# Moving one DMA, one mean and one sum in a convolution kernel whose two main engines are nearly equal

## The reference, cut to what matters

```python
xp = log_pooling(x)      # 12 masks of 9x9 (averages over rings and sectors), stacked as a 4x3 block per pixel
out = conv(xp, w_conv1, stride=(4, 3))        # so: 12 products of 256x256 per pixel
out = out + conv(x, w_center) + b_center      # 1x1, the pixel itself
mean = out.mean(axis=(0, 2, 3)); var = out.var(axis=(0, 2, 3))
out = (out - mean) * rsqrt(var + 1e-5) * gamma + beta
return relu(out + x)                           # x: 32 images, 256 channels, 28 x 28, float32
```

## Time and profile before

| What | us |
|---|---|
| Median of 3 runs | 1618.82 (1618.82 to 1619.4) |
| The profiled execution, its own time | 1618.86 |
| Its span, first to last instruction | 1617.2 |
| TensorE (PE) busy | 1461.5 |
| VectorE (DVE) busy | 1443.0 |
| ScalarE (ACT) busy | 658.6 |
| POOL busy | 121.0 |

### The profile page before, as it was taken

One profiled execution on the slowest core, in us unless ns is written; L12 is line 12 of the kernel. 1 busy time (PEld: TensorE's weight loads), 2 busy tenths in 40 slices (PEclk: granted clock), 3 DMA queues, 4 the chain that ended last, 5 costly groups with the idle time before them and its releaser, 6 DMA issues.

```text
span 1617.2 us, 22814 instructions
## 1 busy us (share of the span) xinstructions
PE 1461.5 (90%) x8518; PEld 1458.7 (90%) x8518; DVE 1443.0 (89%) x1327; ACT 658.6 (41%) x721; POOL 121.0 (7%) x160
## 2 busy tenths in 40 slices
PE   9999999999999999999999999999999999993000
PEld 9899999999999999999999999999999999993000
DVE  8999999999999999999999999999999999996432
ACT  3334444444333444434343344433434344444432
POOL 1000000000000000000000000000000000000000
PEclk9999999999999999999999999999999999996555
DMA  7355555565455555555545555455554566579999
GB/s 222 88 133 140 144 129 129 131 147 131 122 120 134 147 137 128 127 133 140 131 113 123 145 146 136 125 127 139 137 126 110 132 147 158 155 237 424 425 425 402
DMA packets 65352, 268.76 MB, mean 166 GB/s; under 512 B 7616, under 2 KB 7616, under 8 KB 65344
## 3 DMA queue, kind: packets, MB, share of 16 engines
q1 hardware_dynamic: 39744, 160.53, 30.3%
q0 software_dynamic: 20736, 82.45, 25.7%
q10 hardware_dynamic: 4864, 25.69, 3.8%
HBM read 218.07 MB, written 50.58 MB: 166 GB/s over the span
## 4 chain that ended last, share of the span: by engine, by line
PE 83%; DVE 5%; DMA 4%; ACTq 3%; ACT 3%; issue 1%; SPq 0%; DVEq 0%; POOLq 0%
PE acc L724 28%; PE acc L725 28%; PE acc L723 28%; ACTq L462 3%; ACT phase L459 2%; DMA phase<-y_dram 2%; DVE phase L467 1%; DMA ends<-x_wide 1%; DVE pooled_split L468 1%; DMA row<-x_wide 1%; DMA out<-phase 1%; ACT m_copy L416 0%; DVE y_stage L467 0%; DVE inner_split L468 0%; DVE row L467 0%
## 5 line engine op out<-in xcount | busy, mean ns | idle before, releaser
L398 ACT ACTIVATE pooled_split<-phase 128x1456 fp32r<-128x1456 f32 x192 | 274.1, 1428 | 637.7 <-DVE phase L467 637.2
L468 DVE TENSOR_TENSOR pooled_split<-phase,pooled_split 128x1456 fp32r<-128x1456 f32 x192 | 315.1, 1668 | 0.3 <-ACT pooled_split L398 0.3
L723 PE MATMUL acc<-pooled_split,w_first 128*128 128x364 f32 x768 | 252.3, 329 | 1.5 <-DVE pooled_split L468 1.4
L724 PE MATMUL acc<-pooled_split,w_first 128*128 128x364 f32 x768 | 252.9, 329 | 0.0
L725 PE MATMUL acc<-pooled_split,w_first 128*128 128x364 f32 x768 | 252.8, 329 | 0.0
L725 PE MATMUL acc<-pooled_split,w_outer 128*128 128x364 f32 x768 | 252.7, 329 | 0.0
L723 PE MATMUL acc<-pooled_split,w_outer 128*128 128x364 f32 x768 | 252.1, 328 | 0.5 <-DVE pooled_split L468 0.5
L724 PE MATMUL acc<-pooled_split,w_outer 128*128 128x364 f32 x768 | 252.5, 329 | 0.0
L723 PE MATMUL acc<-inner_split,w_inner 128*128 128x392 f32 (+1 forms) x640 | 216.4, 338 | 3.0 <-DVE w_inner L510 3.0
L723 PE MATMUL acc<-inner_split,w_first 128*128 128x392 f32 (+1 forms) x640 | 217.8, 340 | 0.7 <-DVE inner_split L468 0.5
L725 PE MATMUL acc<-inner_split,w_inner 128*128 128x392 f32 (+1 forms) x640 | 217.3, 340 | 0.0
(11 more groups left out here) (82 smaller groups left out, 2222.6 us busy)
## 6 DMA issues: line engine op xcount, KB each, us to landing
row<-x_wide SPq DMA_DIRECT2D x64, 558.0 KB, 3.7
row<-x_wide POOLq DMA_DIRECT2D x64, 558.0 KB, 7.5
ends<-x_wide SPq DMA_DIRECT2D x64, 504.0 KB, 3.9
ends<-x_wide POOLq DMA_DIRECT2D x64, 504.0 KB, 6.5
x_pad<-x SPq DMA_DIRECT2D x64, 392.0 KB, 3.1
y_dram<-y_stage SPq DMA_DIRECT2D x31, 784.0 KB, 5.5
phase<-y_dram SPq DMA_DIRECT2D x30, 784.0 KB, 23.6
out<-phase ACTq DMA_DIRECT2D x30, 784.0 KB, 33.3
```

Source lines behind the costliest of these rows:

```text
L398: nc.scalar.activation(view(pooled_split, 2 * j * PAIR, (1, PAIR)), view(phase2, POOLED_LOW + 2 * j * PAIR, (1, PAIR)), ACT.Copy)\
L468: sub = lambda out_, a, b: nc.vector.tensor_tensor(out_, a, b, ALU.subtract)
L723: nc.tensor.matmul(place, hi_w, hi_in, start=start, stop=False)
L724: nc.tensor.matmul(place, lo_w, hi_in, start=False, stop=False)
```

## The change

Three edits. The first image's ends load now goes out ahead of the outer weights of c = 0 and ahead of SP's wait for row2_ready. The pivot is made by ScalarE in the first half of image 1 (image_steps with second=True), with two passes of the function Identity, scale -1/784 and accum_out, one for each output group, and the four measure passes of image 0 stand where those of later images do. And in second halves three_columns is called ahead of lo_of_sums, for all images but the first.

```diff
@@ the loads before the loops
             begin_sum(0, 0, row2, W + 3, row2_begun)
+            begin_sum(0, 0, ends, W, ends_begun)
+            sp.wait_ge(row2_ready, 16)
             load_weights(0, 1)
-            sp.wait_ge(row2_ready, 16)
-            begin_sum(0, 0, ends, W, ends_begun)
             load_x(0, 1)
@@ ScalarE
+            def make_pivot():
+
+                for o in range(CH):
+                    act.wait_ge(y_ready, o + 1 + FREE)
+                    wait_from_one(act, pivot_ready, o)
+                    nc.scalar.activation(view(m_copy, 0, (1, HW)), view(y_stage, o * HW, (1, HW)), ACT.Identity,
+                                         scale=-1.0 / HW, accum_out=minus_pivot[:, o:o + 1])\
+                        .then_inc(pivot_ready, 1)
@@ ScalarE, image_steps
-                    if c == 1 and not first and not second:
+                    if c == 1 and not first:
                         measure(image - 1, 1)
...
                     for j in range(PAIRS):
                         split_pooled(s, j)
-                        if second and c == 1 and j > 0:
-                            measure(image - 1, j - 1)
-                    if c == 0 and not first and not second:
+                    if second and c == 0:
+                        make_pivot()
+                    if c == 0 and not first:
                         measure(image - 1, 0)
@@ VectorE, image_steps
                     if c == 0:
                         take_middle(image - 1)
-                    lo_of_sums(s)
-                    three_columns(image, c)
+                        lo_of_sums(s)
+                        three_columns(image, c)
+                    else:
+                        three_columns(image, c)
+                        lo_of_sums(s)
                     lo_of_shifted(s)
...
-                    if second and c == 1:
-                        make_pivot()
                     third_sum(s)
```

More of the change, by code:

```diff
@@ L153, in x_slot_whole @@
             return view(phase2, (2 * d - 1) * PLACE, (HW, CH), (1, HW))
-        pivot_stats = sb("pivot_stats", CH * 2 * 6)
-        pivot_moments = sb("pivot_moments", CH * 2)
         minus_pivot = sb("minus_pivot", CH)
@@ L409, in copy_middle @@
                         .then_inc(m_copied, 1)
+            def make_pivot():
[5 more added lines that the diff above has]
+                        .then_inc(pivot_ready, 1)
             def measure(image, o):
                 act.wait_ge(y_ready, CH * image + o + 1 + FREE)
-                act.wait_ge(pivot_ready, 1)
+                act.wait_ge(pivot_ready, CH)
                 for kind, function in enumerate((ACT.Identity, ACT.Square)):
@@ L531, in take_y @@
                     add(y, view(acc, 2 * o * BANK, (BANK, 2), (H, U), (1, H)), y).then_inc(y_ready, 1)
[L533 to L543, removed]
             def pooled_place(s, j, first, *dims):
@@ L689, in _ @@
             dve.wait_ge(params_loaded, 48)
-            dve.wait_ge(pivot_ready, 1)
+            dve.wait_ge(pivot_ready, CH)
             link(sub(mean[:, :], totals[:, 0:CH], minus_pivot[:, :]))
```

## The result

The changed kernel takes 1624.63 us (median of 8 runs, 1622.8 to 1627.37) against 1619.32 for the kernel before (8 runs): a ratio of 1.0033, 95% interval [1.0023, 1.0044], or 5.3 us slower (forecast: 4.3 slower). Its profiled execution took 1627.37 us, the slowest of the eight, with a span of 1625.7.

What follows compares the result with a forecast made beforehand. TensorE and VectorE shared the lead; VectorE, with 1.02 us to spare per image, would become the loop's bound. TensorE's end moves from 1468.4 to 1472.7: 1618.86 + 4.3 = 1623.2 us, range 1616.8 to 1628.0.

Steps and rivals of the forecast that it cites:

- Third edit: Second halves: a 1.58 us wait for inner_split becomes about 2.8 us for row sums; VectorE bounds the loop.
- The step of take_y: From image 2 on, VectorE's take_y stands about 45.25 us apart, against TensorE's 45.08.
- L - S: Second halves: landing of the accumulated row sums (L) minus start of the last differences instruction, phase<-d (S); mean 3.70 us.
- rival A: Loop: TensorE stays the bound from mean L - S of 3.53 down; not slower, 1616.9 to 1617.8 us; chance 0.27.
- Rival B: Loop: row sums land early enough not to be waited for (L - S about 2.5); faster, 1615.2 us; chance 0.03.
- First edit: Start: ends lands before VectorE needs it, gaining 2.05 us (0.9 to 2.05); the later outer weights cost 0.
- Rival D: Start: the outer weight piece is late by up to 1.1 us, carried to the end, 1624.3 us; chance 0.06.
- the sign of D: Start: ScalarE's first pooled split starting later than 21.8 us would show that the outer weight piece was late.
- Second edit: Image 1, first half: mean on ScalarE takes 2.97 and 0.31 us off VectorE; cost 0 with 0.7 us spare.
- The sum: Whole kernel: take_y of image 2 at 115.66, then 29 cycles, to TensorE's end at 1472.7 against 1468.4, +4.3 us.
- the hole in TensorE adds nothing: Image 1, second half: TensorE finds lo_of_sums done only at 91.5 us, but VectorE doesn't wait for TensorE; cost 0.
- wait for inner_split in nearly every image: Loop: TensorE would wait for inner_split in nearly every image, a few tenths of a us at a time.

Runs made afterwards that it cites:

- e3: Changed kernel with SP's store of y_stage moved from the first half into the second half, behind the x load; 1616.06 us, ratio 0.9981 to the kernel before.
- e8: Changed kernel with SP's store of y_stage ahead of its load of row for the second half, not behind it; 1617.43 us, ratio 0.9988.
- e1: Kernel before with only the third edit, three_columns ahead of lo_of_sums in second halves; 1633.80 us, ratio 1.0087.
- e5: Kernel before with only the first edit, ends of the first image ahead of the outer weights; 1616.62 us, ratio 0.9987.
- e11: Changed kernel with the new order in image 1 only and the old order from image 2 on; 1618.37 us, ratio 0.9995.
- e10: The changed kernel measured again, nothing altered; 1622.87 us, ratio 1.0019 to the kernel before.
- e2: Changed kernel with second halves in the old order, so only the first two edits; 1614.49 us, ratio 0.9970 to the kernel before.
- e12: The kernel of e2 (first two edits, old order in second halves) measured again in another group; 1614.36 us, ratio 0.9970.
- e9: The kernel of e4 again (changed kernel, old order in image 1's second half only), beside the changed kernel on one chip; 1621.79 us, ratio 1.0016.
- e4: Changed kernel with the old order in the second half of image 1 only; 1625.29 us, ratio 1.0036 to the kernel before.
- e7: The kernel of e2 (first two edits, old order) with the store of y_stage moved into the second half; 1614.40 us, ratio 0.9970.

## Why the prediction was right

**Third edit, the sign and the size.** Right, and by its mechanism. The step of take_y was forecast at 45.25 and is 45.31. For every kernel in which VectorE bounds the loop, step less mean L - S is the same: 45.31 - 3.71, 45.43 - 3.84, 45.44 - 3.83, 45.21 - 3.62 and 45.26 - 3.68 all give 41.58 to 41.61. The prediction had 41.55. Where L - S is under 3.5 (e3, e8), the step is TensorE's 45.08. e3 moved one store, kept the new order, and took 8.6 us of the loss away; e8 moved the same store elsewhere and took 5 to 7. This shows that the landing, not the order as such, is the cause. That the time came within 1.4 us of the forecast is in part luck: with the mean L - S of 3.84 that e1 had, it would have been some 4 us longer. The row sums' landings in the changed kernel (mean 3.71) were what the trace of before had said (3.69), so idle VectorE did not make them earlier: rival A had its place right (it decides at about 3.5) and its condition did not come true in the new order as it stands. Rival B's condition, an L - S of about 2.5, came true in e3 (2.35), and there 1616.06 stands against B's 1615.2. By a rule of the Trainium skill (SBUF — State Buffer, Who interferes with whom) a VectorE instruction with two inputs in SBUF and a GpSimd instruction that reads SBUF block each other. The prediction asked whether that could make the landings earlier beside an idle VectorE, though the same section of the Trainium skill tells of a probe in which tensor_tensor, the instruction that VectorE runs here, did not stall a DMA. No run here shows such a gain: POOL issues them while VectorE is busy in both kernels, and from issue to landing it is 7.82 us before and 7.87 after.

**First edit.** Right: 2.05 forecast, 2.0 at VectorE (25.51 in place of 27.53, with no wait ahead of it), and 2.2 us in the time when alone (e5). ScalarE's timeline in the changed kernel shows the outer weights just in time:

```profile
18.70 1.59 ACT L382 ACTIVATE w_first<-w_stage 128x512 fp32r<-128x512 f32 x2 [5.53 <-DMA w_stage<-w_raw]
21.91 2.96 ACT L396 ACTIVATE pooled_split<-phase 128x1456 fp32r<-128x1456 f32 x2 [1.63 <-DVE phase L474]
```

It waits 5.53 us for them, starts at 18.70 and is done 1.6 us before its pooled split. Rival D did not come. The split does start at 21.91 and not at 21.8, which the prediction had named as the sign of D, but what it waits for there is VectorE's phase and not the weights: the sign was too sharp by 0.1 us.

**Second edit.** Right in the cost: six passes that ScalarE can hide.

```profile
79.99 0.84 ACT L414 ACTIVATE m_copy<-y_stage 128x784 f32<-128x784 f32 x1
...
83.99 0.19 ACT L423 ACTIVATION_READ_ACCUMULATOR m_copy<-y_stage,minus_pivot 128x1 f32 x1
85.02 1.51 ACT L387 ACTIVATE inner_split<-phase 128x1568 fp32r<-128x1568 f32 x1 [0.85 <-DVE phase L474]
```

The four of them that stand between the halves, with their reads of the sums, take it from 79.99 to 84.18, and 0.85 us later the inner split starts, when v_ready comes (0.7 forecast).

**The step that was off: the start.** The sum put take_y of image 2 at 115.66; it came at 117.71. 0.6 us of this is image 1's landing: the row sum starts at 88.28 in place of 87.67. The other 1.4 us is the sentence that the hole in TensorE adds nothing because VectorE doesn't wait for TensorE there. VectorE did wait: 0.22 us at 105.74 and 1.16 us at 117.71. What the prediction had left out is the clock. It gave TensorE 22.54 us for the half behind the hole, and was right about the hole: in e11, where the hole is 2.4 us and the clock stays at 1.00, that half takes TensorE 22.66 us (from 91.68 to the first matmul of image 2 at 114.34), no wait for TensorE stands ahead of take_y, and it comes at 115.67. In the changed kernel, with 5.9 us of the half at 0.50, it takes 25.34 (92.17 to 117.51). With e11's 22.66 us it would have been ready at about 114.8 (an estimate, 92.17 + 22.66), before VectorE got there at 116.55. e10 repeats this: a hole of 2.6 us, half clock, a wait of 1.15 us, take_y at 117.43.

The other misses are small: 29 steps took 1313.95 us against 1313.1, and image 31's landing was 0.4 later. Together they make about 3.4 us for the profiled execution (TensorE done at 1476.1, forecast 1472.7), which is also the slowest of the eight; the median is 1.4 above the forecast.

**A detail that failed.** I expected TensorE to wait for inner_split in nearly every image. The profile lists six such waits, 6.4 us in all, of which 2.9 are in image 1 and 1.7 in image 31. Since TensorE was late from image 1 on, it began the second half of image 2 only 1.4 us behind the end of lo_of_sums, and this took up VectorE's lag of 0.23 us an image until image 8. From there on it begins within 0.4 us of lo_of_sums, and waits show in some images only.

**Where the gain of the first two edits went.** They are worth 4.8 us (e2), and the third edit gives back 8 to 10 (changed kernel and e10 against e2 and e12). 0.1 us in the mean L - S is worth 3 us. With the means of one kernel's profiled executions between 3.68 and 3.71, of all kernels with this store in place between 3.62 and 3.84, the cost of the third edit has no exact size: the changed kernel was 5.3 us slower than before in the first comparison and 4.0 in the second (e10).

## What to carry to other kernels

Where two engines have nearly the same cycle, price an exchange of two instructions by what each waits for at its new place: here a 1.6 us wait for an engine was traded for a 2.8 us wait for a DMA that the old order had hidden, and 1 us of spare time per image was all there was. Look up the landing of every transfer that a moved instruction needs, in all passes of the loop, and compare it with its new start. And if a reorder fails on a landing, look at what is queued ahead of that transfer before giving it up: moving one store brought the landing 1.4 us forward.

## What the runs showed that I had not expected

With a landing on the critical path the time itself is less steady: eleven runs of the changed kernel (e10) lay within 5.5 us of each other, those of e9 within 2.1, and e4 and e9, the same kernel in two groups, 3.5 apart; seven runs without a landing on the path (e12) lay within 1.1, and e2 and e12 0.1 apart. How much of e10's spread is the landing, and how much image 1's clock, is not shown. An accumulating DMA of 558 KB took 7.9 us from issue to landing behind a store of 784 KB issued 0.7 us ahead of it, and 6.4 to 6.5 with the store moved (e3, e7, e8), on average. A store 3.2 us ahead of a load on the same queue did not delay that load (POOL issued 4.32 us behind SP in both). And the length of a hole in TensorE did not tell whether the clock would fall: the hole of 2.9 us in the changed kernel and the one of 2.6 in e10 were followed by 6.8 us at half clock, those of 2.4 in image 1 of e1 and e11 by none, but e1's next one, 2.4 us too, and one of 2.2 us in image 31 of e8 by 3.4 us.
